# The queries' up product as two row tiles of the array, and the experts' turned rows and sums in one PSUM bank

## The chip, the cores and the metric

The kernel is one program on one core of a Trainium2 chip. Its time is the device time of one execution in microseconds. The engines are PE (TensorE, matmul), ACT (ScalarE), DVE (VectorE), POOL (GpSimd) and SP (SyncE, here the engine that issues most transfers). PSUM, which PE writes and ACT and DVE read, has eight banks of 128 partitions x 512 floats.

## The reference, cut to what matters

Two transformer layers over 4 x 256 tokens of 256 features, in float32. Layer 0 adds an attention and a mixture of experts, both of the same normed input. The parts that the change touches:

```python
xn = _layernorm(x)
# attention of layer 0: 16 heads of 128, through a narrow waist of 64
q = (h @ Wq_c @ Wq_up).reshape(b, t, H, D).transpose(0, 2, 1, 3)   # Wq_c 256x64, Wq_up 64x2048
q = rmsnorm(apply_partial_rope(q, cos, sin), q_norm_w)
... # sliding-window and block attention on q, then two output products
# experts of layer 0: 32 experts, 6 for each token
out += g[:, None] * (jnp.maximum(xf @ w1 + b1, 0.0) @ w2 + b2)      # w1 256x176, w2 176x256
```

Layer 1 has a linear attention and eight experts, two for each token; the change does not alter its work.

## The kernel before

Tokens lie in eight tiles of 128. After a prologue (norms, routing, shared experts, keys) PE, ACT and DVE go through steps g = -1 to 9 in `attention_pe`, `attention_act` and `attention_dve`. In step g the tile g+1 gets its queries, tile g-1 is turned and scored, tile g-2 gets probabilities turned and values, and tile g-3 is projected. A step has eight places: four k places (k = 0 to 3) and four s places (s = 0 to 3, one for each quarter of the tile). Each place also holds one beat of the experts, 79 tiles of 128 gathered rows in a pipeline (`BEATS`, `expert_pe`, `expert_act`). The order is written out by hand and each engine follows its own.

At beat i, PE turns the gathered rows of expert tile i (L865, bank 1), computes the first expert product of tile i-2 (L875, bank 5), and the second, the sums, of tile i-4 (L883 and L884, bank 3, columns 0 to 255). ACT copies the turned rows out (L892), applies the relu (L899, L900), and copies the sums out with the gate as scale (L907). POOL gathers tile i+4 (L837) and adds tile i-4 to the sums in memory (L845); L907 waits for an earlier add to free its buffer.

At place k, in PE's order: the experts' beat, four transposes of tile g-1's queries (`turn_queries`, L499, bank 0), a quarter of the projection (L540, bank 7), one up product of 128 x 512 of tile g+1 (`up_queries`, L486, bank 0), at k=2 the first turned probabilities (L522), and in step 0 a quarter of a fold of two weights (L549). On ACT: the beat, the copy of the turned queries (L592), square and copy of the up product (L586, L587), at k=1 the exponentials of the blocks (L609, L610), at k=2 the copy of turned probabilities (L617). Turned queries and up products share bank 0, so each waits for ACT's copy of the other.

At place s, PE has scores (L511), values (L532), the next turned probabilities (L522), and then the beat; ACT has tanh and exp (L601, L603), the copy of the values (L624), of the turned probabilities (L617), and then the beat. DVE masks and sums there (L698 to L704), and at s=0 sums the squares of all new queries (L665), for which it waits for all four up products' copies.

The up product contracts over 64 features only; the operands `QCT` and `WQ` have 128 partitions, and POOL sets the other 64 to zero in the prologue (L1557, L1558), so that the whole array is used in every matmul. A float32 matmul is two matmul instructions and two weight loads in the trace.

Of the kernel before, what the change touches and what calls it, by code (L numbers as in the profile page):

```python
# [16 lines left out]
P = 128  # L17
B, S, HID = 4, 256, 256
T = B * S
NT = T // P  # L20
# [9 lines left out]
NSUB = 4  # L30
# [94 lines left out]
def build(nc, a, out):  # L125
# [5 lines left out]
    with ctx:  # L131
# [95 lines left out]
        WQC = cut1(KC * QC)  # L227
# [252 lines left out]
        def up_queries(pe, t, k):  # L480

            if t >= 2:
                pe.wait_ge(t_sb, (t - 2) * NG + k + 1)
            else:
                wait(pe, q_ev, t * NG + k)
            nc.tensor.matmul(ps[0][:, :], QCT[:, t * P:(t + 1) * P], wq3[:, k, :], start=True, stop=True).then_inc(q_ps, 1)  # L486

        def turn_queries(pe, t, k):
# [3 lines left out]
            ahead = t + 2 if k else t + 1  # L492
            if ahead < NT:
                pe.wait_ge(q_ev, ahead * NG + (k or NG))
            else:
                wait(pe, t_sb, t * NG + k)
            q3 = v3(QB[t % 2], H)
            for h in range(4):
                ins = nc.tensor.transpose(ps[0][:, h * P:(h + 1) * P], q3[:, 4 * k + h, :], IDN[:, :])  # L499
            ins.then_inc(t_ps, 1)  # L500

        def scores(pe, t, s):
# [5 lines left out]
            for hg in range(NG):  # L508
                if s == 0:
                    pe.wait_ge(t_sb, t * NG + hg + 1)  # L510
# [42 lines left out]
        def attention_pe(pe, g):  # L553
            for k in range(NG):
# [6 lines left out]
                if on(g + 1):  # L561
                    up_queries(pe, g + 1, k)
# [16 lines left out]
        def take_queries(act, t, k):  # L579

            act.wait_ge(q_ps, t * NG + k + 1)
            if k == 0:
                wait(act, qss, t)
                if t == 1:
                    act.wait_ge(x_st, 16)
            nc.scalar.activation(SQ[:, k * 512:(k + 1) * 512], ps[0][:, :], ACT.Square)  # L586
            nc.scalar.activation(QB[t % 2][:, k * 512:(k + 1) * 512], ps[0][:, :], ACT.Copy).then_inc(q_ev, 1)  # L587

        def take_queries_T(act, t, k):

            act.wait_ge(t_ps, t * NG + k + 1)
            nc.scalar.activation(qt4[:, :, 4 * k:4 * k + 4, :].transpose([0, 2, 1, 3]),  # L592
                                 ps[0][:, :].rearrange("p (h s r) -> p h s r", h=4, s=NSUB), ACT.Copy).then_inc(t_sb, 1)
# [36 lines left out]
        def attention_act(act, g):  # L630
            for k in range(NG):
# [4 lines left out]
                if on(g + 1):  # L636
                    take_queries(act, g + 1, k)
# [220 lines left out]
        def expert_pe(pe, i):  # L858

            g = i  # L860
            if g < NT0:
                pe.wait_ge(gathered[g % 4], 16 * (g // 4 + 1))
                wait(pe, xT_sb, g)
                for k in range(KC):
# [14 lines left out]
            if g >= 0:  # L879
                pe.wait_ge(hT_sb, g + 1)  # L880
                wait(pe, y_sb, g)
                w, hT = w2t[g % NW], hT0[g % NHT]
                nc.tensor.matmul(ps[3][:, 0:HID], hT[0:DHB, 0:P], w[0:DHB, 0:HID], start=True, stop=False)  # L883
                nc.tensor.matmul(ps[3][:, 0:HID], hT[0:DHB + 1, P:2 * P], w[0:DHB + 1, HID:2 * HID], start=False, stop=True).then_inc(y_ps, 1)  # L884

        def expert_act(act, i):
# [15 lines left out]
            if g >= 0:  # L902
# [4 lines left out]
                nc.scalar.activation(yt0[g % 2], ps[3][:, 0:HID], ACT.Copy, scale=GY[:, g:g + 1]).then_inc(y_sb, 1)  # L907
# [6 lines left out]
        def turn_tokens(pe, t):  # L914
            pe.wait_ge(xn_ok, NT + t + 1)
            wait(pe, x1t_sb, t - 1)
# [494 lines left out]
        with nc.Block() as block:  # L1411
            @block.sync
            def _(sp):
# [15 lines left out]
                sp.dma_start(WQ[0:QC, :], a["L0_attn_Wq_up"]).then_inc(ld_ct, 16)  # L1429
# [44 lines left out]
                for i in range(NBEAT):  # L1474
# [30 lines left out]
                    if i == NBEAT - 4:  # L1505
                        sp.wait_ge(q_ps, NT * NG)
# [41 lines left out]
            def _(pool):  # L1548
# [8 lines left out]
                ready.link(nc.gpsimd.memset(QCT[QC:, :], 0.0))  # L1557
                ready.link(nc.gpsimd.memset(WQ[QC:, :], 0.0))  # L1558
# [43 lines left out]
            def _(act):  # L1602
# [26 lines left out]
                for n in range(2):  # L1629
                    act.wait_ge(qc_ps, n + 1)  # L1630
                    nc.scalar.activation(QCT[0:QC, n * 512:(n + 1) * 512], ps[4 + n][0:QC, :], ACT.Copy).then_inc(qc_sb, 1)
# [8 lines left out]
                act.wait_ge(const_set, 5 + NHT)  # L1640
# [13 lines left out]
            def _(dve):  # L1654
# [39 lines left out]
                dve.wait_ge(ld_ct, 16 * 4)  # L1694
# [69 lines left out]
            def _(pe):  # L1764
# [160 lines left out]
```

## Time and profile before

| | us |
|---|---|
| median of three runs | 608.5 |
| lowest and highest run | 606.54, 614.78 |
| profiled execution, its time | 607.58 |
| its span | 605.5 |

The profile is of one execution. Busy times are of engines; PE's matmuls overlap at their ends, so that the distance of two starts, not the duration, says what a matmul costs when they follow each other. PEld is the weight load, beside PE. In a timeline row the first number is the start, the second the duration of the group (xN instructions), and the bracket is the idle time of that engine just before and what ended it. The granted clock is TensorE's, as a share of its full speed.

### The profile page before, as it was taken

The numbers are of one execution on the slowest core, as the hardware profiler recorded it, in microseconds if no ns is written. First come the engines' busy times: TensorE is split into PE (matmuls) and PEld (weight loads), VectorE is DVE, ScalarE is ACT, GpSimd is POOL, SyncE is SP. The second block draws the span as 40 slices with busy tenths as digits, with TensorE's granted clock in tenths as the row PEclk, the third lists the DMA queues.
The fourth block names the chain that finished last, engine by engine and source line by source line (L and its number), as shares of the span: only waits on it lengthen the run. The fifth ranks groups of instructions, "written<-read, shape, count | busy, mean of one in ns | idle before, by whom it ended". The sixth has DMA issues, their size and how long they took to land.

```text
span 605.5 us, 9516 instructions
## 1 busy us (share of the span) xinstructions
PE 534.5 (88%) x2887; PEld 403.2 (67%) x2887; DVE 336.9 (56%) x884; ACT 313.0 (52%) x739; POOL 330.7 (55%) x237
## 2 busy tenths in 40 slices
PE   0898999699778999999999999999979998899961
PEld 0654777588566788788787887888757454466641
DVE  3389843324065381743917439151565976998733
ACT  0215226365564766766667666575622228666530
POOL 3100437868667586675866758654311024888770
PEclk9999999899897999999999999999999999999995
DMA  9940628886886986575775757865377012556766
GB/s 286 344 166 6 162 59 208 196 163 174 218 252 164 235 214 141 118 173 120 151 160 118 172 120 156 188 134 112 36 233 236 1 35 62 79 87 94 97 77 216
DMA packets 87200, 90.31 MB, mean 149 GB/s; under 512 B 26672, under 2 KB 75248, under 8 KB 86704
## 3 DMA queue, kind: packets, MB, share of 16 engines
q1 hardware_dynamic: 66528, 61.44, 35.7%
q0 software_dynamic: 19584, 27.24, 26.5%
q10 hardware_dynamic: 1040, 1.05, 0.5%
q8 instruction: 24, 0.39, 0.3%
q14 instruction: 24, 0.20, 0.1%
HBM read 65.25 MB, written 22.60 MB: 145 GB/s over the span
## 4 chain that ended last, share of the span: by engine, by line
PE 56%; DVE 15%; issue 8%; DMA 8%; POOL 7%; ACT 5%; SPq 0%; POOLq 0%; DVEq 0%
PE bank L540 9%; DMA expert_sums<-expert_weights,token_of_slot 6%; PE bank L875 6%; PE bank L1115 4%; PE bank L486 4%; PE bank L883 3%; PE bank L884 3%; POOL expert_sums L845 3%; PE bank L511 3%; POOL expert_weights L837 3%; PE bank L532 3%; PE bank L1785 3%; PE bank L1133 2%; PE bank L499 2%; PE bank L865 1%
## 5 line engine op out<-in xcount | busy, mean ns | idle before, releaser
L845 POOL DMA_INDIRECT expert_sums<-expert_weights,token_of_slot x79 | 129.6, 1641 | 57.9 <-ACT expert_weights L907 35.4
L837 POOL DMA_INDIRECT expert_weights<-normed_x,token_of_slot x79 | 91.8, 1162 | 112.3 <-DVE token_of_slot L366 46.6
L875 PE MATMUL bank<-expert_weights 128*88 128x128 f32 x632 | 83.6, 275 | 0.5 <-issue 0.4
L875 PEld LDWEIGHTS bank<-expert_weights 128*88 128x88 f32 x632 | 74.3, 159 | 0.9 <-issue 0.9
L540 PE MATMUL bank<-out_weights,expert_weights 128*128 128x256 f32 x256 | 60.1, 380 | 1.4 <-ACT expert_weights L624 1.4
L907 ACT ACTIVATE expert_weights<-bank,chosen_bf 128x256 f32<-128x256 f32 x79 | 37.5, 475 | 33.0 <-issue 18.7
L1083 POOL DMA_INDIRECT expert_sums<-expert_weights,token_of_slot x23 | 45.8, 1989 | 14.4 <-DMA expert_sums<-expert_weights,token_of_slot 5.5
L883 PE MATMUL bank<-expert_weights 88*128 88x256 f32 x158 | 48.0, 385 | 6.0 <-ACT expert_weights L907 5.0
L698 DVE SCALAR_TENSOR_TENSOR expert_weights<-bank,blocks_valid 128x64 f32<-128x64 f32 x32 | 7.1, 221 | 81.0 <-ACT expert_weights L601 80.4
L540 PEld LDWEIGHTS bank<-out_weights,expert_weights 128*128 128x128 f32 x256 | 46.5, 190 | 8.2 <-ACT expert_weights L624 3.1
L1076 POOL DMA_INDIRECT tiles<-normed_x,token_of_slot x23 | 25.2, 1097 | 41.6 <-DVE token_of_slot L1070 28.9
L884 PE MATMUL bank<-expert_weights 89*128 89x256 f32 x158 | 47.4, 380 | 0.0
L1115 PE MATMUL bank<-expert_weights,tiles 128*128 x92 | 44.1, 601 | 1.3 <-DVE tiles L1165 0.9
L511 PEld LDWEIGHTS bank<-keys,expert_weights 128*128 128x128 f32 x256 | 33.8, 196 | 14.9 <-issue 13.9
L511 PE MATMUL bank<-keys,expert_weights 128*128 128x112 f32 x256 | 34.7, 280 | 8.4 <-DVE expert_weights L698 8.4
L486 PE MATMUL bank<-q_up_weights,qc_T 128*128 128x512 f32 x64 | 35.4, 635 | 7.3 <-ACT expert_weights L592 5.8
L586 ACT ACTIVATE tiles<-bank 128x512 f32<-128x512 f32 x32 | 19.1, 596 | 42.7 <-PE bank L486 40.3
L853 DVE SCALAR_TENSOR_TENSOR expert_weights<-expert_weights,chosen_before_bf 128x6 f32<-128x6 f32 x79 | 15.9, 222 | 42.9 <-DMA expert_weights<-normed_x,token_of_slot 42.6
L892 ACT ACTIVATE expert_weights<-bank 128x256 f32<-128x256 f32 x79 | 30.3, 384 | 11.9 <-PE bank L865 11.9
L899 ACT ACTIVATE expert_weights<-bank,expert_weights 88x128 f32<-88x128 f32 x79 | 28.8, 364 | 13.2 <-PE bank L875 8.4
L532 PE MATMUL bank<-expert_weights 112*128 112x512 f32 x64 | 33.4, 603 | 2.3 <-ACT expert_weights L617 2.3
L884 PEld LDWEIGHTS bank<-expert_weights 89*128 89x128 f32 x158 | 30.3, 192 | 4.4
(278 smaller groups left out, 1110.3 us busy)
## 6 DMA issues: line engine op xcount, KB each, us to landing
expert_weights<-experts_out SPq DMA_DIRECT2D x79, 192.8 KB
expert_weights<-experts_in SPq DMA_DIRECT2D x79, 176.0 KB
expert_weights<-L_ffn_wi SPq DMA_DIRECT2D x32, 128.0 KB
expert_weights<-w_comp SPq DMA_DIRECT2D x1, 2048.0 KB, 10.9
expert_weights<-fold_g SPq DMA_DIRECT2D x1, 2048.0 KB, 16.2
expert_sums<-zeros SPq DMA_DIRECT2D x2, 1024.0 KB, 13.3
expert_weights<-L_ffn_wo SPq DMA_DIRECT2D x16, 128.0 KB
normed<-expert_sums SPq DMA_DIRECT2D x2, 1024.0 KB, 5.7
```

The costliest lines, as they stand in the source:

```text
L486: nc.tensor.matmul(ps[0][:, :], QCT[:, t * P:(t + 1) * P], wq3[:, k, :], start=True, stop=True).then_inc(q_ps, 1)
L511: ins = nc.tensor.matmul(ps[2][:, hg * NKEY:(hg + 1) * NKEY], QT[:, s * H * NSR + hg * P:s * H * NSR + (hg + 1) * P], kwin[:, b, i, :], st ...
L532: nc.tensor.matmul(ps[6][:, :], VW[b % 2][0:NKEY, i * D:(i + 1) * D], PTB[s % 2][0:NKEY, :], start=True, stop=True).then_inc(pv_ps, 1)
L540: ins = nc.tensor.matmul(ps[7][:, 0:HID], AO[:, h * P:(h + 1) * P], wc3[:, h, :], start=(h == 0), stop=(h == H - 1))
L837: nc.gpsimd.indirect_dma_start(xt0[g % 4], None, xn0, bass.IndirectOffsetOnAxis(ap=MAP[:, g:g + 1], axis=0)).then_inc(gathered[g % 4], 16)
L845: nc.gpsimd.indirect_dma_start(sums0[g % 2], bass.IndirectOffsetOnAxis(ap=MAP[:, g:g + 1], axis=0), yt0[g % 2], None, compute_op=ALU.add). ...
L875: ins = nc.tensor.matmul(ps[5][0:DHB, c * P:(c + 1) * P], w[:, k * DH + c * DHB:k * DH + (c + 1) * DHB], xT0[g % NXT][:, k * P:(k + 1) * P ...
L883: nc.tensor.matmul(ps[3][:, 0:HID], hT[0:DHB, 0:P], w[0:DHB, 0:HID], start=True, stop=False)
L884: nc.tensor.matmul(ps[3][:, 0:HID], hT[0:DHB + 1, P:2 * P], w[0:DHB + 1, HID:2 * HID], start=False, stop=True).then_inc(y_ps, 1)
L907: nc.scalar.activation(yt0[g % 2], ps[3][:, 0:HID], ACT.Copy, scale=GY[:, g:g + 1]).then_inc(y_sb, 1)
L1083: nc.gpsimd.indirect_dma_start(sums1[n % 2], bass.IndirectOffsetOnAxis(ap=MAP[:, g:g + 1], axis=0), yt1[g % 4], None, compute_op=ALU.add). ...
L1115: ins = nc.tensor.matmul(ps[HB[g % 2]][:, :], xT1[g % 3][:, k * P:(k + 1) * P], w[:, 0, k * 2 * MI:(k + 1) * 2 * MI], start=(k == 0), stop ...
```

## The change

- The waist's product is computed twice, side by side: `w_qc` holds `Wq_c` two times, so that `QCT` has the 64 features in partitions 0 to 63 and again in 64 to 127. `WQ` holds the weights of heads 0 to 7 in its first 64 partitions and those of heads 8 to 15 in the other 64, in half the columns. The two memsets are gone.
- `up_queries` runs at k=1 and k=3 only. Each call is four products of 64 rows and 256 columns, in turn from the lower and the upper 64 partitions, into banks 0 and 3. One signal follows the fourth. ACT then takes bank 0 and bank 3, a square and a copy each (`take_queries` with i = 0, 1).
- The queries are turned in the order of head groups 0, 2, 1, 3, with banks 0 and 3 in turn; the scores follow that order.
- To free bank 3, the experts' sums go to columns 256 to 511 of bank 1, whose first half holds the turned rows. PE waits for the previous sum's copy (`y_sb`) ahead of the turned rows, and for this beat's copy of the turned rows (`xT_sb`) ahead of the sums.
- `WQC` lies in the free half of `WQ`; some semaphore counts follow, and PE waits for `slots_ok` ahead of the steps and for the last sum ahead of layer 1's turned tokens.

```diff
-        wq3 = v3(WQ[:, :], NG)
+        QBANK, QORDER = (0, 3), (0, 2, 1, 3)
...
-        def up_queries(pe, t, k):
+        def up_queries(pe, t, j):
 
             if t >= 2:
-                pe.wait_ge(t_sb, (t - 2) * NG + k + 1)
+                pe.wait_ge(t_sb, (t - 2) * NG + 2 * j + 2)
             else:
-                wait(pe, q_ev, t * NG + k)
-            nc.tensor.matmul(ps[0][:, :], QCT[:, t * P:(t + 1) * P], wq3[:, k, :], start=True, stop=True).then_inc(q_ps, 1)
+                wait(pe, q_ev, t * NG + 2 * j)
+            for lo in range(0, 512, HID):
+                for i in range(2):
+                    rows = slice(i * QC, (i + 1) * QC)
+                    ins = nc.tensor.matmul(ps[QBANK[i]][:, lo:lo + HID], QCT[rows, t * P:(t + 1) * P], WQ[rows, j * 512 + lo:j * 512 + lo + HID],
+                                           start=True, stop=True)
+            ins.then_inc(q_ps, 1)
 
         def turn_queries(pe, t, k):
...
-            ahead = t + 2 if k else t + 1
+            ahead, part = (t + 1, 3 + k) if k < 2 else (t + 2, k - 1)
             if ahead < NT:
-                pe.wait_ge(q_ev, ahead * NG + (k or NG))
+                pe.wait_ge(q_ev, ahead * NG + part)
...
-                ins = nc.tensor.transpose(ps[0][:, h * P:(h + 1) * P], q3[:, 4 * k + h, :], IDN[:, :])
+                ins = nc.tensor.transpose(ps[QBANK[k % 2]][:, h * P:(h + 1) * P], q3[:, 4 * QORDER[k] + h, :], IDN[:, :])
...
-                if on(g + 1):
-                    up_queries(pe, g + 1, k)
+                if k % 2 and on(g + 1):
+                    up_queries(pe, g + 1, k // 2)
...
-        def take_queries(act, t, k):
-
-            act.wait_ge(q_ps, t * NG + k + 1)
-            if k == 0:
+        def take_queries(act, t, j, i):
+
+            k = j + 2 * i
+            act.wait_ge(q_ps, t * 2 + j + 1)
+            if i + j == 0:
...
-            nc.scalar.activation(SQ[:, k * 512:(k + 1) * 512], ps[0][:, :], ACT.Square)
-            nc.scalar.activation(QB[t % 2][:, k * 512:(k + 1) * 512], ps[0][:, :], ACT.Copy).then_inc(q_ev, 1)
+            nc.scalar.activation(SQ[:, k * 512:(k + 1) * 512], ps[QBANK[i]][:, :], ACT.Square)
+            nc.scalar.activation(QB[t % 2][:, k * 512:(k + 1) * 512], ps[QBANK[i]][:, :], ACT.Copy).then_inc(q_ev, 1)
...
-                if on(g + 1):
-                    take_queries(act, g + 1, k)
+                if k % 2 and on(g + 1):
+                    for i in range(2):
+                        take_queries(act, g + 1, k // 2, i)
...
@@ expert_pe @@
                 wait(pe, xT_sb, g)
+                wait(pe, y_sb, g - 4)
...
                 wait(pe, y_sb, g)
+                pe.wait_ge(xT_sb, min(i + 1, NT0))
                 w, hT = w2t[g % NW], hT0[g % NHT]
-                nc.tensor.matmul(ps[3][:, 0:HID], hT[0:DHB, 0:P], w[0:DHB, 0:HID], start=True, stop=False)
-                nc.tensor.matmul(ps[3][:, 0:HID], hT[0:DHB + 1, P:2 * P], w[0:DHB + 1, HID:2 * HID], start=False, stop=True).then_inc(y_ps, 1)
+                nc.tensor.matmul(ps[1][:, HID:], hT[0:DHB, 0:P], w[0:DHB, 0:HID], start=True, stop=False)
+                nc.tensor.matmul(ps[1][:, HID:], hT[0:DHB + 1, P:2 * P], w[0:DHB + 1, HID:2 * HID], start=False, stop=True).then_inc(y_ps, 1)
...
@@ turn_tokens, prologue @@
+            pe.wait_ge(y_sb, NT0)
...
-                sp.dma_start(WQ[0:QC, :], a["L0_attn_Wq_up"]).then_inc(ld_ct, 16)
+                for i in range(2):
+                    sp.dma_start(WQ[i * QC:(i + 1) * QC, 0:H * D // 2], a["L0_attn_Wq_up"][:, i * H * D // 2:(i + 1) * H * D // 2]).then_inc(ld_ct, 16)
...
-                ready.link(nc.gpsimd.memset(QCT[QC:, :], 0.0))
-                ready.link(nc.gpsimd.memset(WQ[QC:, :], 0.0))
...
-                        ins = nc.tensor.matmul(ps[4 + n][0:QC, :], wqc3[:, k, :], xnT3[:, k, n * 512:(n + 1) * 512],
+                        ins = nc.tensor.matmul(ps[4 + n][:, :], wqc3[:, k, :], xnT3[:, k, n * 512:(n + 1) * 512],
...
-    c["w_qc"] = rows(g("attn_Wq_c"), KC)
+    c["w_qc"] = rows(np.concatenate([g("attn_Wq_c")] * 2, 1), KC)
```

## Rows read from the trace of the kernel before

**Rows 1.** The page: busy time of each engine, with its share of the span

```profile
PE 534.5 (88%) x2887; PEld 403.2 (67%) x2887; DVE 336.9 (56%) x884; ACT 313.0 (52%) x739; POOL 330.7 (55%) x237
```

**Rows 2.** Windows: start:end, us, busy per engine, granted clock, DMA share, GB/s

```profile
100.00:120.00 20.00, 14.32 (x73) 10.71 (x72) 9.26 (x19) 7.21 (x22) 17.23 (x11) 0.91 0.89 204
...
320.00:360.00 40.00, 39.06 (x242) 32.28 (x241) 21.85 (x60) 27.39 (x68) 26.81 (x18) 1.00 0.61 134
```

**Rows 3.** The chain that ended last, two steps' first projection: start, us, what

```profile
300.82 1.73 PE bank L540 x8
...
338.58 1.73 PE bank L540 x8
```

**Rows 4.** Waits from 85 to 200 us: who for whom, total, times, longest

```profile
DVE expert_weights L853 <- DMA expert_weights<-normed_x,token_of_slot: 40.8, 12, 8.2
```

**Rows 5.** The page's groups: the up product of the queries

```profile
L486 PE MATMUL bank<-q_up_weights,qc_T 128*128 128x512 f32 x64 | 35.4, 635 | 7.3 <-ACT expert_weights L592 5.8
```

**Rows 6.** Timeline, PE across a beat's border: start, us, engine, line

```profile
307.38 1.02 PE L486 MATMUL bank<-q_up_weights,qc_T 128*128 128x512 f32 x2
308.24 0.38 PE L865 MATMUL bank<-ident,expert_weights 128*128 128x128 f32 x2
...
309.34 0.60 PE L883 MATMUL bank<-expert_weights 88*128 88x256 f32 x2
309.77 0.60 PE L884 MATMUL bank<-expert_weights 89*128 89x256 f32 x2
```

**Rows 7.** The same timeline, ACT behind that up product

```profile
308.44 0.60 ACT L586 ACTIVATE tiles<-bank 128x512 f32<-128x512 f32 x1 [1.99 <-PE bank L486]
...
309.41 0.42 ACT L609 ACTIVATE expert_weights<-expert_weights 128x256 f32<-128x256 f32 x1
...
309.82 0.38 ACT L892 ACTIVATE expert_weights<-bank 128x256 f32<-128x256 f32 x1
```

**Rows 8.** Timeline, ACT and PE after the fourth up product of a step

```profile
318.86 0.60 ACT L586 ACTIVATE tiles<-bank 128x512 f32<-128x512 f32 x1 [1.99 <-PE bank L486]
...
319.83 0.50 ACT L601 ACTIVATE expert_weights<-bank 128x384 f32<-128x384 f32 x1
...
321.74 0.39 ACT L892 ACTIVATE expert_weights<-bank 128x256 f32<-128x256 f32 x1
...
321.94 0.60 PE L883 MATMUL bank<-expert_weights 88*128 88x256 f32 x2
```

**Rows 9.** Timeline, last beat of the step and the next beat's first instruction

```profile
332.22 1.12 PE L511 MATMUL bank<-keys,expert_weights 128*128 128x112 f32 x8 [0.94 <-DVE expert_weights L698]
...
334.80 0.38 ACT L892 ACTIVATE expert_weights<-bank 128x256 f32<-128x256 f32 x1
...
335.15 0.60 PE L883 MATMUL bank<-expert_weights 88*128 88x256 f32 x2
...
336.02 0.38 PE L865 MATMUL bank<-ident,expert_weights 128*128 128x128 f32 x2
...
336.22 0.47 ACT L907 ACTIVATE expert_weights<-bank,chosen_bf 128x256 f32<-128x256 f32 x1 [0.25 <-PE bank L884]
```

**Rows 10.** Timeline, PE restarting behind ACT in the stage without project

```profile
159.22 0.60 ACT L592 ACTIVATE expert_weights<-bank 128x512 f32<-128x512 f32 x1
...
159.87 1.13 PE L486 MATMUL bank<-q_up_weights,qc_T 128*128 128x512 f32 x2 [0.69 <-ACT expert_weights L592]
...
161.93 0.60 PE L883 MATMUL bank<-expert_weights 88*128 88x256 f32 x2
...
191.40 1.12 PE L486 MATMUL bank<-q_up_weights,qc_T 128*128 128x512 f32 x2 [0.69 <-issue]
```

**Rows 11.** Timeline, a restart after a longer pause of PE

```profile
154.19 2.08 PE L486 MATMUL bank<-q_up_weights,qc_T 128*128 128x512 f32 x2 [1.81 <-ACT expert_weights L592]
...
157.71 0.60 PE L883 MATMUL bank<-expert_weights 88*128 88x256 f32 x2
```

**Rows 12.** Window of the same stretch

```profile
154.00:157.00 3.00, 2.81 (x7) 1.67 (x8) 0.23 (x2) 0.83 (x3) 2.56 (x2) 0.50 0.81 162
```

More of the change, by code:

```diff
@@ L226, in build @@
         KWR = cut1(D)[0:NB * B]
-        WQC = cut1(KC * QC)
+        WQC = WQ[:, H * D // 2:H * D // 2 + 2 * KC * QC]
         WGS = cut1(H * HID)
@@ L491, in turn_queries @@
                 pe.wait_ge(qn, t + 1)
-            ahead = t + 2 if k else t + 1
+            ahead, part = (t + 1, 3 + k) if k < 2 else (t + 2, k - 1)
             if ahead < NT:
-                pe.wait_ge(q_ev, ahead * NG + (k or NG))
+                pe.wait_ge(q_ev, ahead * NG + part)
             else:
-                wait(pe, t_sb, t * NG + k)
+                wait(pe, t_sb, t * NG + k - 1)
             q3 = v3(QB[t % 2], H)
             for h in range(4):
-                ins = nc.tensor.transpose(ps[0][:, h * P:(h + 1) * P], q3[:, 4 * k + h, :], IDN[:, :])
+                ins = nc.tensor.transpose(ps[QBANK[k % 2]][:, h * P:(h + 1) * P], q3[:, 4 * QORDER[k] + h, :], IDN[:, :])
             ins.then_inc(t_ps, 1)
@@ L507, in scores @@
             b, i = t // TPB, t % TPB * NSUB + s
-            for hg in range(NG):
+            for n, hg in enumerate(QORDER):
                 if s == 0:
-                    pe.wait_ge(t_sb, t * NG + hg + 1)
+                    pe.wait_ge(t_sb, t * NG + n + 1)
                 ins = nc.tensor.matmul(ps[2][:, hg * NKEY:(hg + 1) * NKEY],
@@ L585, in take_queries @@
                     act.wait_ge(x_st, 16)
-            nc.scalar.activation(SQ[:, k * 512:(k + 1) * 512], ps[0][:, :], ACT.Square)
-            nc.scalar.activation(QB[t % 2][:, k * 512:(k + 1) * 512], ps[0][:, :], ACT.Copy).then_inc(q_ev, 1)
+            nc.scalar.activation(SQ[:, k * 512:(k + 1) * 512], ps[QBANK[i]][:, :], ACT.Square)
+            nc.scalar.activation(QB[t % 2][:, k * 512:(k + 1) * 512], ps[QBANK[i]][:, :], ACT.Copy).then_inc(q_ev, 1)
         def take_queries_T(act, t, k):
             act.wait_ge(t_ps, t * NG + k + 1)
-            nc.scalar.activation(qt4[:, :, 4 * k:4 * k + 4, :].transpose([0, 2, 1, 3]),
-                                 ps[0][:, :].rearrange("p (h s r) -> p h s r", h=4, s=NSUB), ACT.Copy).then_inc(t_sb, 1)
+            nc.scalar.activation(qt4[:, :, 4 * QORDER[k]:4 * QORDER[k] + 4, :].transpose([0, 2, 1, 3]),
+                                 ps[QBANK[k % 2]][:, :].rearrange("p (h s r) -> p h s r", h=4, s=NSUB), ACT.Copy).then_inc(t_sb, 1)
         def probs(act, t, s):
@@ L906, in expert_act @@
                 act.wait_ge(gate_ok, g + 1)
-                nc.scalar.activation(yt0[g % 2], ps[3][:, 0:HID], ACT.Copy, scale=GY[:, g:g + 1]).then_inc(y_sb, 1)
+                nc.scalar.activation(yt0[g % 2], ps[1][:, HID:], ACT.Copy, scale=GY[:, g:g + 1]).then_inc(y_sb, 1)
         def in_ring(tiles, length, r):
@@ L1630, in _ @@
                     act.wait_ge(qc_ps, n + 1)
-                    nc.scalar.activation(QCT[0:QC, n * 512:(n + 1) * 512], ps[4 + n][0:QC, :], ACT.Copy).then_inc(qc_sb, 1)
+                    nc.scalar.activation(QCT[:, n * 512:(n + 1) * 512], ps[4 + n][:, :], ACT.Copy).then_inc(qc_sb, 1)
                 shared_relu(4)
@@ L1853, in _ @@
                 expert_pe(pe, 3)
-                pe.wait_ge(ld_ct, 16 * 4)
-                pe.wait_ge(const_set, 5 + NHT)
+                pe.wait_ge(ld_ct, 16 * 5)
+                pe.wait_ge(const_set, 3 + NHT)
                 pe.wait_ge(qc_sb, 2)
@@ L1860, in _ @@
                 pe.wait_ge(ld_wg, 32)
+                pe.wait_ge(slots_ok, 2)
                 for g in range(FIRST_STEP, LAST_STEP):
```

6 lines of the change are left out of this document (3 added, 3 removed).

## The prediction

> **What bounds the kernel now.** I read the page first: PE is busy for 88% of the span, DVE, ACT and POOL for 52 to 56% [rows 1]. Then windows of 20 to 40 us, to see where PE has slack. Between 100 and 120 us it is busy 14.3 of 20 us while POOL is busy 17.2 and the DMA engines 0.89; from 85 to 200 us the gates wait 40.8 us for gathered tiles, so that stretch is paced by gathers and scatter-adds. From about 200 us on PE is full: 39.06 of 40 us, ACT at 27.4 [rows 2, 4]. Last the timeline of one beat there. PE runs without a hole: the up product takes 0.86 (307.38 to 308.24), the next beat's turned rows and first expert product 1.10 (to 309.34), then the expert's output pair starts [rows 6]. So in the attention steps g=2 to 7 (from about 190 us on) a hole in PE is a hole in the total, and a shorter product is a gain. The chain of waits runs through PE's products here, and gives the period of a step of eight beats: the first projection stands at 300.82 and at 338.58, 37.8 us [rows 3].
>
> **The profiled execution** took 607.58 us, its span 605.5; the sum goes against 607.6, 0.9 below the median of 608.5.
>
> **The products.** 32 of them run as 64 instructions of 512 columns [rows 5], 0.43 each, 0.86 a product; a step has four, 3.44 us. Afterwards a step has two groups, each of four products of 64 rows and 256 columns, that is eight instructions. A 256-column instruction occupies 0.43/2 = 0.217 [rows 6]. No row shows two row tiles side by side, so I bound a group. Below: perfect pairing, 4 x 0.217 = 0.87. Above: no overlap, 8 x 0.217 = 1.73, plus a drain of PE at each change of shape; a drain is the tail of a matmul, 0.60 less 0.43 = 0.17 [rows 6], so 2.07. I take 1.2: each product is two instructions on the same rows, which I assume not to run beside each other, so that only the three borders between the tiles can overlap: five slots, 1.08, and about one tail. A step saves 3.44 - 2.4 = 1.04; the bounds are 1.70 saved and 0.70 lost.
>
> The Trainium skill (TensorE: Matmul & The Clock Gate, Part 3) says that matmuls of different row groups start some 4 ns apart; by that a group is the 0.87. The Trainium skill (TensorEngine Tiling (Array Packing), Key Properties) says against the change that a switch of tiling mode drains the engine; by that the tails belong in the sum, twice. No row here shows either.
>
> **ACT's burst, the largest term.** Before, each beat left ACT one bank: L586 and L587, 0.97 together (318.86 to 319.83 [rows 8]). Now k=1 and k=3 leave two banks behind one signal, which comes after the whole group: four evacuations, 1.94. They stand ahead of the next beat's L892 in ACT's queue. That was harmless: nothing in the same beat needed L892. The shared bank changes this, since the expert's output pair now waits for this beat's L892. At k=1: ACT starts 0.20 after the products' end (308.44 against 308.24), needs 1.94, then 0.41 for the blocks' exponentials (309.41 to 309.82 [rows 7]), then L892, 0.39. PE restarts behind ACT 0.15 late: L592 ends at 159.82 and PE starts 0.05 later, and from there to L883 it takes 2.06 where 1.96 is usual [rows 10, 6]. That is 3.09 after the products; PE is there after 1.10. **Hole 1.99.**
>
> At k=3, ACT was without a pause from 318.86 to L892 at 321.74; 0.97 later it ends at 323.10, PE restarts at 323.25 instead of 321.94 [rows 8]. **Hole 1.31.** The following two beats each add 0.18, as below, but the fourth scores waited 0.94 for DVE [rows 9], whose chain moves by 1.31 itself; so 1.31 is what passes. In the last beat L892 ends at 335.18, restart 335.33 against 335.15: **0.18** [rows 9]. The beat after the first turned probabilities, k=2, has the same order, another **0.18**.
>
> **The new wait of the turned rows** for the previous sum: free where attention work lies between two beats. Between the last beat of a step and the first of the next nothing does: L907 starts at 336.22, ends at 336.69, restart 336.84 against 336.02 [rows 9]. **0.82.**
>
> A full step: 1.99 + 1.31 + 0.18 + 0.18 + 0.82 = 4.48 added, 1.04 saved, 3.44 net. There are four (g=3 to 6): **+13.8**.
>
> **g=2** has no projection between turning and up: the four up products wait some 0.7 to 0.8 each for L592 [rows 10], 3.0 in all; two such waits of 0.69 remain. At k=0 the turn covers 0.44 of the wait for L907: 0.20 + 0.47 + 0.15 - 0.44 = 0.38. So 4.48 + 1.38 + 0.38 - 3.0 - 1.04 = **+2.2**. **g=7** has no up products: five beats at 0.18 and 0.82, **+1.7**.
>
> **g=-1 to 1** I take at nothing: gathers and scatter-adds pace them [rows 2, 4], and holes in PE fall into time in which it would wait anyway. In g=0 the fold, eight instructions of 0.216 behind every up group, covers most of the burst. If that cover is thinner, the first step's four full beats cost 0.8 each and g=1 about 2, so +5; if the saved product time shows there, -2.
>
> **At no cost:** the two memsets gone from POOL (it waits for the routing long after), two loads of 64 partitions for one, the doubled weights of the compression (512 columns hide the wider load), the waits for `slots_ok` and, in layer 1, for the last sum: all done long before. Bounds 0.5 either way. The turn order 0, 2, 1, 3 moves nothing: the same copies at the same beats. SP's and POOL's queues issue the same transfers.
>
> **Sum:** 607.6 + 13.8 + 2.2 + 1.7 = 625.3, and 0.9 for the median: **626 us**, 2.9% slower. Two per cent, about what a measurement can tell, ends at 620.7 and 596.3.
>
> **Rivals.**
> *Full pairing, and ACT's second hole absorbed:* groups at 0.87 gain 0.66 a step over my choice, and if PE's hole at k=3 falls into waits for DVE, 1.3 goes too. For it: DVE does hold PE up by 0.94 a step. Against: DVE waits for the same ACT queue. Five steps x 1.96 = 9.8, so 616, within 2%. Its first half is what the Trainium skill's page on the clock gate states, above. Chance 0.24.
>
> *The clock falls at each long hole:* after a pause of 1.81 us the granted clock was 0.50 of full speed, which is the level of 1.2 GHz [rows 11, 12]; from L486 to L883 it took 3.52 instead of 2.06, 1.46 lost. The hole at k=1 is as long. Five of them: +7.3, 633. Against: this is one pause; after those of 0.69 and 0.94 the next products ran at full pace [rows 9, 10], and the hole at k=3 is nearer to these. The Trainium skill (TensorE: Matmul & The Clock Gate, Part 1) has the clock fall after idle time, a rule against the change. Chance 0.14.
>
> *Faster:* the evacuation turns out not to be on PE's path, because PE's work ahead of the output pair outlasts ACT's. It decides where that work exceeds 3.1 us behind a group; it is 1.10 in full steps and 2.8 with a fold. Then all 16 groups show, at 0.87: 16 x 0.85 = 13.6, so 595. Only the order of ACT's queue could be otherwise than I read it. Chance 0.07.
>
> *My forecast*, 618 to 635 by itself: 0.55. Slower 0.55 + 0.14 = 0.69, within 0.24, faster 0.07. The range 611 to 638 leaves out the faster case and the edges of the two outer ones.
>
> **What would show it.** Behind each second group four evacuations of 0.49 run back to back on ACT, and L883 waits for L892 about 2.0 us at k=2 and 1.3 us at the first scores beat; L865 waits 0.8 for L907 once a step; PE's share from 320 to 360 us falls from 0.98 to about 0.88; the period grows from 37.8 to about 41. The start of one group and the next instruction are 1.2 us apart if five slots are right, 0.87 or over 1.7 if not. I am wrong if L883 shows no wait for L892, or if steps g=2 to 7 are no longer while the early stage is.

## The result: 3.5% slower, and the profile after

The median went from 611.42 us (606.54 to 614.78, four runs, taken in the same comparison) to **630.98 us** (628.41 to 631.75, four runs): ratio **1.0354**, 95% interval 1.0317 to 1.0391. The profiled execution took 630.83 us, its span 629.0; before 607.58 and 605.5. So the difference is 19.6 between the medians and 23.5 between the two spans, and the accounts below are of the spans. Ratios leave out the few executions that ran longer at a lower granted clock.

In the kernel after, the up product is L489, turned rows L873, first expert product L883, the sums L892 and L893; on ACT the copy of turned rows is L901, the copy of the sums L916, square and copy of the up product L592 and L593, the copy of the turned queries L598. Experiments have line numbers of their own, a few lines apart.

The page after, busy times as in [rows 1]:

```profile
PE 537.3 (85%) x2951; PEld 404.0 (64%) x2951; DVE 335.1 (53%) x884; ACT 317.7 (51%) x739; POOL 327.2 (52%) x235
```

PE is not busier, only spread over 23.5 us more. The window that answers to the second of [rows 2], and one in step g=2:

```profile
320.00:360.00 40.00, 36.21 (x228) 29.18 (x227) 20.46 (x56) 25.03 (x61) 24.85 (x16) 1.00 0.59 133
204.00:206.00 2.00, 2.00 (x11) 2.00 (x10) 0.00 (x0) 1.45 (x4) 1.41 (x2) 0.50 0.58 174
```

From 320 to 360 us PE's share fell from 39.06 to 36.21 of 40 us at full clock. What it waited for, the whole span (who for whom: total, times, longest):

```profile
PE bank L892 <- ACT expert_weights L901: 19.2, 16, 1.7
...
PE bank L873 <- ACT expert_weights L916: 13.6, 16, 3.7
```

The first line is the new wait: the sums for this beat's copy of the turned rows. The timeline shows how it comes about. First the beat behind the group at k=1 of a full step (start, duration, engine, line; the bracket is the idle time before):

```profile
318.61 1.89 PE L545 MATMUL bank<-out_weights,expert_weights 128*128 128x256 f32 x8
...
320.43 1.13 PE L489 MATMUL bank<-q_up_weights,qc_T 64*128 64x256 f32 x8
321.49 0.44 PE L873 MATMUL bank<-ident,expert_weights 128*128 128x128 f32 x2
321.61 0.60 ACT L592 ACTIVATE tiles<-bank 128x512 f32<-128x512 f32 x1 [2.21 <-PE bank L489]
321.77 1.04 PE L883 MATMUL bank<-expert_weights 128*88 128x128 f32 x8
322.10 0.59 ACT L593 ACTIVATE normed<-bank 128x512 f32<-128x512 f32 x1
322.58 0.60 ACT L592 ACTIVATE tiles<-bank 128x512 f32<-128x512 f32 x1
323.06 0.62 ACT L593 ACTIVATE normed<-bank 128x512 f32<-128x512 f32 x1
323.54 0.44 ACT L615 ACTIVATE expert_weights<-expert_weights 128x256 f32<-128x256 f32 x1
...
323.95 0.40 ACT L901 ACTIVATE expert_weights<-bank 128x256 f32<-128x256 f32 x1
...
324.50 0.67 PE L892 MATMUL bank<-expert_weights 88*128 88x256 f32 x2 [1.69 <-ACT expert_weights L901]
```

From the start of the turned rows behind the group to L892 it takes 321.49 to 324.50, 3.01, where it took 1.10 [rows 6]. Then the group at k=3 and the first scores beat, and the scores and the end of the beat at the last place:

```profile
332.46 1.14 PE L489 MATMUL bank<-q_up_weights,qc_T 64*128 64x256 f32 x8
333.52 1.15 PE L516 MATMUL bank<-keys,expert_weights 128*128 128x112 f32 x8
...
337.51 0.39 ACT L901 ACTIVATE expert_weights<-bank 128x256 f32<-128x256 f32 x1
...
338.04 0.67 PE L892 MATMUL bank<-expert_weights 88*128 88x256 f32 x2 [0.96 <-ACT expert_weights L901]
```

```profile
307.18 1.12 PE L516 MATMUL bank<-keys,expert_weights 128*128 128x112 f32 x8 [0.30 <-DVE expert_weights L705]
...
310.28 0.67 PE L892 MATMUL bank<-expert_weights 88*128 88x256 f32 x2
...
311.42 0.47 ACT L916 ACTIVATE expert_weights<-bank,chosen_bf 128x256 f32<-128x256 f32 x1 [0.50 <-PE bank L893]
312.04 0.41 PE L873 MATMUL bank<-ident,expert_weights 128*128 128x128 f32 x2 [0.66 <-ACT expert_weights L916]
```

Where the time lies, by the starts of the experts' sums on PE (start of tile 8n to start of tile 8(n+1); four full steps together):

| | before | after | difference | forecast |
|---|---|---|---|---|
| up to the first sum | 88.98 | 87.08 | -1.90 | 0 |
| g=-1 | 26.35 | 30.38 | +4.03 | |
| g=0 | 35.51 | 35.03 | -0.48 | |
| g=1 | 38.41 | 39.35 | +0.94 | g=-1 to 1: 0 |
| g=2 | 34.65 | 38.97 | +4.32 | +2.2 |
| g=3 to 6 | 150.95 | 164.76 | +13.81 | +13.8 |
| g=7 | 33.16 | 35.36 | +2.20 | +1.7 |
| behind | | | +0.6 | 0 |

### The profile page after: what moved, and what is told of

Same layout as the page of the kernel before. It is cut to its first block, busy times and chain, and to the rows that moved or that the text cites. A ratio compares the mean times of both kernels' runs of the same rounds, so it can differ in the third digit from the quotient of the medians.

```text
span 629.0 us, 9647 instructions
## 1 busy us (share of the span) xinstructions
PE 537.3 (85%) x2951; PEld 404.0 (64%) x2951; DVE 335.1 (53%) x884; ACT 317.7 (51%) x739; POOL 327.2 (52%) x235
## 3 DMA queue, kind: packets, MB, share of 16 engines
q10 hardware_dynamic: 1040, 1.05, 0.5%
## 4 chain that ended last, share of the span: by engine, by line
PE 63%; DVE 14%; ACT 10%; issue 6%; DMA 5%; POOL 1%; SPq 0%; ACTq 0%; POOLq 0%; DVEq 0%
PE bank L545 9%; PE bank L883 8%; PE bank L892 6%; PE bank L893 5%; PE bank L1125 4%; DMA expert_sums<-expert_weights,token_of_slot 3%; PE bank L516 3%; PE bank L489 3%; PE bank L537 3%; PE bank L873 2%; ACT normed L593 2%; PE bank L554 2%; PE bank L1794 2%; PE bank L1143 2%; PE bank L504 2%
## 5 line engine op out<-in xcount | busy, mean ns | idle before, releaser
L844 POOL DMA_INDIRECT expert_weights<-normed_x,token_of_slot x79 | 89.1, 1128 | 124.7 <-DVE token_of_slot L366 47.6
L883 PE MATMUL bank<-expert_weights 128*88 128x128 f32 x632 | 85.0, 278 | 0.4 <-ACT expert_weights L909 0.4
L883 PEld LDWEIGHTS bank<-expert_weights 128*88 128x88 f32 x632 | 75.6, 161 | 0.7 <-issue 0.7
L892 PE MATMUL bank<-expert_weights 88*128 88x256 f32 x158 | 51.8, 410 | 20.1 <-ACT expert_weights L901 19.2
L916 ACT ACTIVATE expert_weights<-bank,chosen_bf 128x256 f32<-128x256 f32 x79 | 37.6, 475 | 45.6 <-PE bank L893 36.9
L893 PE MATMUL bank<-expert_weights 89*128 89x256 f32 x158 | 47.7, 382 | 0.0
L873 PE MATMUL bank<-ident,expert_weights 128*128 128x128 f32 x158 | 32.0, 285 | 14.3 <-ACT expert_weights L916 13.6
L901 ACT ACTIVATE expert_weights<-bank 128x256 f32<-128x256 f32 x79 | 30.5, 386 | 26.2 <-PE bank L873 26.0
L892 PEld LDWEIGHTS bank<-expert_weights 88*128 88x128 f32 x158 | 24.3, 194 | 28.7 <-issue 28.0
L873 PEld LDWEIGHTS bank<-ident,expert_weights 128*128 128x128 f32 x158 | 19.7, 145 | 28.6 <-issue 26.8
```

Source lines behind the costliest of these rows:

```text
L844: nc.gpsimd.indirect_dma_start(xt0[g % 4], None, xn0, bass.IndirectOffsetOnAxis(ap=MAP[:, g:g + 1], axis=0)).then_inc(gathered[g % 4], 16)
L873: ins = nc.tensor.transpose(ps[1][:, k * P:(k + 1) * P], xt0[g % 4][:, k * P:(k + 1) * P], IDN[:, :])
L883: ins = nc.tensor.matmul(ps[5][0:DHB, c * P:(c + 1) * P], w[:, k * DH + c * DHB:k * DH + (c + 1) * DHB], xT0[g % NXT][:, k * P:(k + 1) * P ...
L892: nc.tensor.matmul(ps[1][:, HID:], hT[0:DHB, 0:P], w[0:DHB, 0:HID], start=True, stop=False)
L893: nc.tensor.matmul(ps[1][:, HID:], hT[0:DHB + 1, P:2 * P], w[0:DHB + 1, HID:2 * HID], start=False, stop=True).then_inc(y_ps, 1)
L916: nc.scalar.activation(yt0[g % 2], ps[1][:, HID:], ACT.Copy, scale=GY[:, g:g + 1]).then_inc(y_sb, 1)
```

## The experiments

Each was timed beside runs of the kernel before on the same chip; a ratio is to these. "Period" is the distance of the sums' starts over a full step (before 37.74, after 41.19; the mean of four steps, in the profiled execution).

### Whole rows instead of row tiles

```diff
-            for lo in range(0, 512, HID):
-                for i in range(2):
-                    rows = slice(i * QC, (i + 1) * QC)
-                    ins = nc.tensor.matmul(ps[QBANK[i]][:, lo:lo + HID], QCT[rows, ...], WQ[rows, ...], ...)
+            for i in range(2):
+                ins = nc.tensor.matmul(ps[QBANK[i]][:, :], QCT[:, t * P:(t + 1) * P], WQ[:, j * 512:j * 512 + 512], ...)
```

> The changed kernel, but each group is two products over all 128 rows and 512 columns into the same two banks, behind the same signal (each query then gets the sum of two head groups' products; this is the part of the computation that is altered). Theory (the loss is ACT's burst and the shared bank, and the row tiles themselves gain): a group costs 1.73 instead of about 1.15 us, some 0.6 in each of 10 to 12 groups on the path, so 631 becomes about 637; the waits of the expert's output pair for the copy of the turned rows stay 2.0 and 1.3 us. Rival (the row tiles cost, by drains at the change of shape): not slower than the changed kernel, 625 to 631.

Measured 644.68 us, ratio 1.054 (1.0495 to 1.0585); the period is 44.15, 2.96 above the kernel after. The row tiles are not what costs. The time is above the 637 that I expected: more went than the products' 1.0, and most of the rest is the clock. PE behind the long hole of this kernel, and a window there:

```profile
335.65 0.67 PE L890 MATMUL bank<-expert_weights 88*128 88x256 f32 x2 [1.82 <-ACT expert_weights L899]
...
336.59 0.95 PE L502 MATMUL bank<-ident,normed 128*128 128x128 f32 x4
337.34 3.26 PE L543 MATMUL bank<-out_weights,expert_weights 128*128 128x256 f32 x8
340.44 0.60 PE L525 MATMUL bank<-ident,expert_weights 128*112 128x128 f32 x4
```

```profile
338.00:340.00 2.00, 2.00 (x6) 1.53 (x6) 0.00 (x0) 0.18 (x1) 1.70 (x2) 0.50 0.71 217
```

Turning and projection take 3.85 (336.59 to 340.44) instead of 2.17 at the same place of the kernel after (325.44 to 327.61). So 1.7 of the 2.96 is the granted clock at 0.50, its lower level of 1.2 GHz; 1.0 is the products, and 0.3 the two long holes, each a little longer (by 0.14 at k=2 and 0.19 at the first scores). The profiled execution was the slowest of five (650.42, mean granted clock 0.962, against 642.28 to 645.91 and 0.972 to 0.978), so the others lost less to the clock than this one.

### The shared bank alone

```diff
 # the kernel before, with nothing changed in the up products
                 wait(pe, xT_sb, g)
+                wait(pe, y_sb, g - 4)
...
+                pe.wait_ge(xT_sb, min(i + 1, NT0))
-                nc.tensor.matmul(ps[3][:, 0:HID], hT[0:DHB, 0:P], ...)
+                nc.tensor.matmul(ps[1][:, HID:], hT[0:DHB, 0:P], ...)
```

> The kernel before with one part of the change, the experts' sums in the second half of bank 1 with both new waits; up products as before. Theory: the expert's output pair waits for this beat's copy of the turned rows even without a burst of four: about 0.6, 1.0, 0.7 and 0.3 us in the four beats behind up products, 0.2 and 0.8 at the end of a step, 3.6 a step, five steps, and 1.7 in the step after: some 20 us, about 629. Rival (the row tiles cost, the bank is free): 606 to 613.

Measured 634.99 us, ratio 1.0392 (1.0351 to 1.0432), period 41.73, +3.99, more than the 3.6 a step and the 629 us that I expected. PE's waits:

```profile
PE bank L885 <- ACT expert_weights L894: 14.2, 30, 0.9
PE bank L866 <- ACT expert_weights L909: 11.4, 12, 2.8
```

This part alone costs as much as the whole change. With one bank of queries left to ACT at each k place the wait comes twice as often (30 times against 16) and is at most 0.9 long: ACT's copy of the turned rows is late in seven of the eight beats of a step, and the pairs gather most of that lateness into two places.

### ACT takes the banks of k=1 behind the copy of the turned rows

```diff
+            def late():
+                for i in range(2):
+                    take_queries(act, g + 1, 0, i)
...
-                    expert_act(act, i)
+                    expert_act(act, i, late if k == 2 and on(g + 1) else None)   # called right behind L901
```

> The changed kernel, but at k=1 ACT takes the two banks behind the next beat's copy of the turned rows instead of ahead of it. Theory: the hole of 2.0 us at k=2 goes, in five steps, and with it the fall of the clock near 205 us: about 619 to 621; the hole of 1.3 at the first scores beat stays. Rival (PE waits for something else there, or another wait takes its place): 628 to 632.

Measured 618.86 us, ratio 1.0128 (1.0088 to 1.0169), period 39.27: 1.92 less. The beat at k=2 in this kernel:

```profile
319.73 1.04 PE L886 MATMUL bank<-expert_weights 128*88 128x128 f32 x8
...
320.73 0.67 PE L895 MATMUL bank<-expert_weights 88*128 88x256 f32 x2
```

Nothing was taken away but the place of four instructions in ACT's queue, and the first of the two holes is gone. That shows it as the cause: same matmuls, same copies, same banks.

### The products not in turn

```diff
-            for lo in range(0, 512, HID):
-                for i in range(2):
+            for i in range(2):
+                for lo in range(0, 512, HID):
```

> The changed kernel, but a group issues both products of the lower rows, then both of the upper rows. Theory of the five slots (instructions of one tile don't overlap, only borders between the tiles do): one border instead of three, seven slots, 1.52 instead of 1.08 us, so a group grows by 0.43 and the total by 4 to 5, about 636. Rival (all overlap, whatever the order; or none does): the same 631.

Measured 628.84 us, ratio 1.0292 (1.025 to 1.0335), not the 636 of the theory of five slots; three full steps take 41.2, and the first takes 42.88. The group takes the same time with both products of the lower rows ahead of both of the upper (318.58 to 319.65):

```profile
318.58 1.14 PE L489 MATMUL bank<-q_up_weights,qc_T 64*128 64x256 f32 x8
319.65 0.44 PE L873 MATMUL bank<-ident,expert_weights 128*128 128x128 f32 x2
```

Cut into its instructions, a group is four pairs in both kernels, and so it is in all 16 groups of each. The two of a pair start 6 to 7 ns apart when issued in turn, and 12 to 14 ns when not. The second pair starts 0.32 behind the first, the next two 0.216 behind each other. In the kernel after, what is left of the group from its third, fifth and seventh instruction on, each row from a narrower window:

```profile
320.75 0.81 PE L489 MATMUL bank<-q_up_weights,qc_T 64*128 64x256 f32 x6
...
320.96 0.60 PE L489 MATMUL bank<-q_up_weights,qc_T 64*128 64x256 f32 x4
...
321.18 0.38 PE L489 MATMUL bank<-q_up_weights,qc_T 64*128 64x256 f32 x2
```

So all eight overlap in twos. "Only the borders between tiles" is wrong, and "in turn" has no part in the gain.

The step of 42.88 is a matter of the clock, behind a hole no longer than those of the other three steps, where the clock stayed at 1.00:

```profile
238.57 0.67 PE L892 MATMUL bank<-expert_weights 88*128 88x256 f32 x2 [1.70 <-ACT expert_weights L901]
...
240.00:242.00 2.00, 2.00 (x7) 1.70 (x6) 0.14 (x2) 0.82 (x2) 1.24 (x2) 0.50 0.42 99
```

### Both pairs moved

The turns go in twos to k=0 and k=2 with the group behind them, and ACT takes each pair of banks one place later, behind the copy of the turned rows:

```diff
+            def turned(k):
+                if k % 2 == 0 and on(g - 1):
+                    turn_queries(pe, g - 1, k)
+                    turn_queries(pe, g - 1, k + 1)
+                if on(g - 3):
+                    project(pe, g - 3, k)
...  # at k=0 turned() stands ahead of the beat, else behind it
-                if k % 2 and on(g + 1):
+                if k % 2 == 0 and on(g + 1):
                     up_queries(pe, g + 1, k // 2)
...  # on ACT
+                    expert_act(act, i, late(k // 2) if k % 2 and on(g + 1) else None)
```

> The changed kernel with its places rearranged: two turns of the queries and the group of products at k=0 and at k=2, ACT takes the two banks at k=1 and k=3 behind the copy of the turned rows, and at k=0 turns and projection stand ahead of the beat. Theory (only ACT's burst ahead of that copy and the uncovered wait for the previous sum cost; the row tiles gain): a full step loses the holes of 2.0, 1.3 and 0.8 us, keeps some 0.2 in the last beat, and gains about 1.2 from the products, so about 1 us a step below the kernel before: 600 to 606. Rival (the shared bank costs wherever it stands): 615 or more.

Measured 607.85 us, ratio 0.9971 (0.994 to 1.0002), period 37.56: the loss is gone, but so is most of the gain, for I had expected 600 to 606 us and a step about 1 us below that of the kernel before. What remains, at each place of scores:

```profile
289.87 1.04 PE L898 MATMUL bank<-expert_weights 128*88 128x128 f32 x8
...
290.97 0.67 PE L907 MATMUL bank<-expert_weights 88*128 88x256 f32 x2
...
292.38 1.12 PE L516 MATMUL bank<-keys,expert_weights 128*128 128x112 f32 x8 [0.30 <-DVE expert_weights L720]
```

L898 to L907 is 1.10 where the work needs 0.88 (321.06 to 321.94 before [rows 8]); ACT's copies of values and probabilities stand ahead of the copy of the turned rows in its queue.

### No squares on ACT

```diff
+            if t == 0:
                 nc.scalar.activation(SQ[:, k * 512:(k + 1) * 512], ps[QBANK[i]][:, :], ACT.Square)
```

> The changed kernel, ACT's squares left out for all tiles but the first (the norms of the queries are then those of the first tile; that is the part left out). Theory: the burst is two copies instead of four operations, 0.97 shorter, so the holes of 2.0 and 1.3 us become 1.0 and 0.3, about 1.9 a step in five steps and no fall of the clock: 619 to 621. Rival (ACT's burst isn't what PE waits for): 630.

Measured 620.54 us, ratio 1.018 (1.0119 to 1.024), period 39.34, 1.85 less. The wait at k=2 fell from 1.69 to 0.71, by the 0.98 of two squares, and the one at the first scores by 0.89:

```profile
315.83 0.67 PE L893 MATMUL bank<-expert_weights 88*128 88x256 f32 x2 [0.71 <-ACT expert_weights L902]
```

Every 0.1 us less on ACT is nearly 0.1 less on PE at these two places, although ACT is busy for only 51% of the span.

### One product on 64 rows, without a partner

```diff
 # the kernel before
-            nc.tensor.matmul(ps[0][:, :], QCT[:, t * P:(t + 1) * P], wq3[:, k, :], ...)
+            nc.tensor.matmul(ps[0][:, :], QCT[0:QC, t * P:(t + 1) * P], wq3[0:QC, k, :], ...)
```

> The kernel before, only with the up product contracting over the 64 partitions that hold data: one row tile, one bank, 512 columns. In the changed kernel the eight instructions of a group start in four pairs some 6 ns apart, whichever way the products are ordered. Theory (a pair is one instruction of each tile): a product on one tile keeps its 0.86 us, perhaps 0.1 to 0.3 for the change of shape, 32 times at most: 608 to 616. Rival (a pair is the two instructions of one 64-row product): a product takes about 0.5 us, 0.35 less in some 24 products on the path: 599 to 603, without any second bank.

Measured 621.12 us, ratio 1.0194 (1.0153 to 1.0235), period 39.18, +1.44, which is 4 x 0.36; 32 x 0.36 is the 11.5 between the medians. That is above both ranges I gave (608 to 616, and 599 to 603 by the rival). Around one such product:

```profile
311.76 1.89 PE L540 MATMUL bank<-out_weights,expert_weights 128*128 128x256 f32 x8
313.59 1.12 PE L486 MATMUL bank<-q_up_weights,qc_T 64*128 64x512 f32 x2
314.64 0.44 PE L865 MATMUL bank<-ident,expert_weights 128*128 128x128 f32 x2
314.91 1.04 PE L875 MATMUL bank<-expert_weights 128*88 128x128 f32 x8
```

Start to start, the projection takes 1.83 instead of 1.73 [rows 3], the product 1.05 instead of 0.86 and L865 0.27 instead of 0.22: 0.34 in all for going to the other shape and back. The two instructions of a lone product don't overlap.

### The copy of the turned rows first in every beat

As with both pairs moved, and at every place L901's counterpart now comes ahead of ACT's copies of the values, at k=3 also ahead of the first turned probabilities':

```diff
                 def run():
+                    if k == 3 and on(g - 2):
+                        probs_T(act, g - 2, 0)
...
+                def take(s=s):
+                    if on(g - 2):
+                        outs(act, g - 2, s)
...
-                    expert_act(act, i)
+                    expert_act(act, i, take)
```

> The rearranged kernel (pairs at k=0 and k=2) with one rule on ACT throughout: the copy of the turned rows goes ahead of whatever else is due in the place (at s places ahead of the copy of the values, at k=3 ahead of the copy of turned probabilities). The rearranged kernel's steps take 37.55 us, with waits of 0.22 us, 0.29 with the restart, left at each s place and 0.1 at k=3. Theory (these waits are on PE's path): a step falls by 0.6 to 0.8 to about 36.9, the step without up products by about 1, in all 4 to 5 us below the rearranged kernel, 602 to 605, ratio to before about 0.99. Rival (DVE's chain through the scores sets the s places, so shorter waits change nothing): steps stay at 37.3 to 37.6 and the total at 607.

Measured **606.27 us**, ratio **0.9935** (0.99 to 0.9971), period 37.01: faster than the kernel before by 0.65%, and the fastest version here. Its window answers to [rows 2]:

```profile
320.00:360.00 40.00, 39.43 (x253) 32.79 (x252) 23.32 (x65) 27.58 (x69) 28.71 (x19) 1.00 0.65 138
```

PE is as full as in the kernel before (39.43 against 39.06), and a step is 0.73 shorter. Not all of the gain comes from there: the first sum starts at 87.26 instead of 88.98, which the missing memsets explain in the main (last experiment).

### The same with whole rows

The edit of the first experiment on the kernel just above.

> The kernel of the run beside it (copy first, pairs at k=0 and k=2), but each group as two products over all 128 rows and 512 columns into the same banks (each query gets the sum of two head groups' products; this is the altered part). What the two row tiles are worth by themselves, with no long hole near them: a group costs 1.71 to 1.73 us instead of 1.20 (four pairs of 0.215 and 0.34 for going to the other shape and back), so a step is 1.0 longer, in five steps and some of the early ones 5 to 6 us. Rival (the 3.0 us a step of the earlier full-row kernel were the row tiles' worth, not the clock's fall): a step 3 longer, 15 in all.

Measured 614.82 us, ratio 1.0058 (1.0023 to 1.0093), period 38.01. The row tiles are worth 38.01 - 37.01 = **1.00 a step**; the clock is at 1.00 here in the window from 320 to 360. The shared bank and the pairs, in this order of ACT's queue, cost 38.01 - 37.74 = 0.27. The medians differ by 8.6, more than the 5 to 6 that the steps give: in the profiled executions 4.1 of the 10.2 between the spans lie behind the last start that the table of steps uses (tile 72), where both kernels issue the same work, at a mean granted clock of 0.93 here and 0.96 there.

### The memsets later

```diff
 # the kernel before
+                pool.wait_ge(xn_ok, NT)      # after all norms
                 ready.link(nc.gpsimd.memset(QCT[QC:, :], 0.0))
```

> The kernel before, with POOL's memsets of QCT and WQ held back until DVE has normed all tokens. In the kernel before, the eight norms of DVE (L398) take 4.86 us beside these memsets, in the changed kernel, without them, 2.67, and the first sum comes 1.9 us earlier. Theory (POOL's memsets slow DVE's norms while both run): the norms take 2.7 us again, the first sum comes 1.5 to 2.2 us earlier than 88.98, and the total falls by 1 to 2, about 608 against 610. Rival (something else in the changed prologue does it, such as the smaller loads): norms at 4.9 us, total as before.

Measured 607.71 us, ratio 0.9958 (0.9923 to 0.9993). The norms beside POOL's memsets, in the kernel before:

```profile
13.25 0.95 POOL L1557 MEMSET qc_T<- 64x1024 f32 x1
13.30 4.86 DVE L398 TENSOR_SCALAR normed<-residual,ln_mean_var,rstd 128x256 f32<-128x256 f32 x8 [2.31 <-POOL rstd L407]
```

and with the memsets held back:

```profile
12.92 2.67 DVE L398 TENSOR_SCALAR normed<-residual,ln_mean_var,rstd 128x256 f32<-128x256 f32 x8 [2.31 <-POOL rstd L407]
...
15.71 0.95 POOL L1558 MEMSET qc_T<- 64x1024 f32 x1 [2.91 <-DVE normed L398]
```

The same eight norms took 2.67 instead of 4.86. The first sum starts at 87.66 (before: 88.98). (The profiled execution took 612.52 in all; its time above the median lies at the end, 200.65 from the sums of tile 72 on, against 197.53 before.) In the three kernels with the memsets where they were it starts at 88.98 to 89.75, in the eight without them at 87.00 to 87.99.

## Why the prediction was right, and by which steps

Forecast 626 us and slower; measured 630.98, inside the range. Against its own profiled execution the sum said +17.7, and the span grew by 23.5. The 5.8 between them are +4.5 in g=-1 to 1, +2.1 in g=2, +0.5 in g=7 and +0.6 behind, less 1.9 in the prologue; that the last of these offsets the others is luck. The full steps, the largest term, were forecast and measured at +13.8.

**What bounds the kernel**: right. From g=2 on every hole of PE came out in the period.

**ACT's burst and the new waits, a full step**: right in place and size. By distances between PE's starts, forecast and measured:

| | forecast | measured |
|---|---|---|
| k=2, sums wait for L901 | 1.99 | 1.90 + 0.07 at the restart |
| first place of scores | 1.31 | 1.23 + 0.07 |
| two middle places of scores, less what the wait for DVE shrank | 0 | 0.61 - 0.61 |
| last beat | 0.18 | 0.18 + 0.07 |
| beat at k=3 | 0.18 | 0.12 + 0.08 |
| L873 waits for L916 | 0.82 | 0.82 |
| beat at k=0 | 0 | 0.03 |
| saved by the products | -1.04 | -1.12 |
| net | 3.44 | 3.45 |

The wait for DVE ahead of the fourth scores went from 0.94 [rows 9] to 0.30 and took up the two middle places, as the forecast had it. Two experiments show the burst as the cause by taking it off: -1.92 by order alone, -1.85 by less work. The shared bank alone brings +3.99. PE's share from 320 to 360 us fell to 0.91, less than to the 0.88 that I named.

**The products**: the size was right by luck, the reason wrong. I had five slots of 0.217 and one tail, 1.2. A group is four full slots, 0.86, and about 0.35 for changing shape and back: 0.09 before it, 0.20 in its own time (0.10 each behind the first and the last pair), 0.06 behind it, or 0.10 where scores follow; 0.34 around the lone product. From the group's start to the next instruction it is 1.06, neither the 1.2 nor the 0.87 that I had named as signs. The Trainium skill (TensorE: Matmul & The Clock Gate, Part 3) has matmuls of different row groups start about 4 ns apart; the trace has 6 to 7 ns in turn and 12 to 14 not in turn, which is next to nothing beside a slot of 216. The Trainium skill (TensorEngine Tiling (Array Packing), Key Properties) has the engine drain when the mode changes; the 0.34 fits that, and is the price that no row of before had. By the first rule alone a group would be the 0.87. The gain, 1.00 a step in the pair of kernels that differ in nothing else, is close to what I took (1.04).

**g=2**: too low, +4.3 for +2.2. Two terms were missing and one was too small. I had the first group wait 0.69 for the turned queries' copy; ACT stood idle for 1.84 ahead of L916, which is ahead of that copy in its queue, and the group waited 2.21. L916 waits for an earlier scatter-add to free its buffer: the one of two tiles before was started by POOL at 190.84 and landed 6.4 later, at 197.2, and L916 starts at 197.31. Then the clock fell. The timeline there:

```profile
197.31 0.47 ACT L916 ACTIVATE expert_weights<-bank,chosen_bf 128x256 f32<-128x256 f32 x1 [1.84 <-issue]
...
198.33 1.13 PE L489 MATMUL bank<-q_up_weights,qc_T 64*128 64x256 f32 x8 [2.21 <-ACT expert_weights L598]
...
202.40 0.67 PE L892 MATMUL bank<-expert_weights 88*128 88x256 f32 x2 [1.69 <-ACT expert_weights L901]
...
203.78 1.02 PE L527 MATMUL bank<-ident,expert_weights 128*112 128x128 f32 x4
...
206.72 0.85 PE L892 MATMUL bank<-expert_weights 88*128 88x256 f32 x2
```

L527 to L892 takes 2.94 where a full step needs 1.65 (327.61 to 329.26), and L892 0.69 instead of 0.51: 1.5 us lost at the lower clock level. The window from 204 to 206 us, above, has it at 0.50. So the rival of the clock came true once of five times. Against these two, the four waits of before were worth 4.0 and not the 3.0 that I took off: in the kernel before the turns of this step take 1.29, 1.39, 1.41 and 1.29 to the next product and each product 0.96, where 0.44 and 0.86 would do. That makes 2.2 + 1.5 + 1.5 - 1.0 = 4.2.

**g=7**: +2.2 for +1.7; five beats at 0.25 instead of 0.18 are 0.35 of the 0.5.

**g=-1 to 1**: +4.5 together, near the upper bound of 5 that I gave, where the sum has nothing. Most is in g=-1, +4.0, and the shared bank alone has +2.4 there (28.75 against 26.35), so the cover by gathers and scatter-adds is thin in that step. The trace shows the main parts. Five times no attention work lies between two beats, and the turned rows wait 0.66 for the previous sum's copy, as in the last beat of a full step: 0.82 each with the restart. Two groups leave a hole of 1.28 for L901, 1.5 each. Some 3.7 of waits that the last beats had before are gone, 1.3 is saved by the products, and 1.1 is the clock at 0.50 in this step's last beat, which in the kernel before comes after the step's end.

**The prologue**: I put the memsets at nothing, for what POOL waits for later. What they cost was not on POOL: they slowed DVE's norms beside them, on the path. -1.9, outside my bound of 0.5; the last experiment shows 1.3 of it.

**The rivals**: full pairing did happen, but its 0.87 was not the price of a group; no hole at k=3 was absorbed, so 616 did not come. The faster case would have needed more than 3 us of PE's work ahead of the sums, and there is 1.1 in the full steps.

## What to carry to other kernels

Where two tenants of one PSUM bank are made to wait for each other's copies, the price of sharing is what stands ahead of these copies in the evacuating engine's queue (3.99 us a step here, and 0.27 with the copy first); put the copy that the matmul engine waits for first, and the rest behind it. An engine at 51% busy can set the time of one at 85%. Two row tiles overlapped in full here, but each visit to the other shape cost 0.35 us, so group the products: a visit of four small products gained 0.5 us, a visit of one lost 0.35.

## What the runs showed of the hardware

- Products of 64 rows on the two halves of the array start 6 to 7 ns apart when issued in turn, and 12 to 14 ns apart when issued one half after the other. Which instruction pairs with which in that order is not settled.
- A lone 64-row product of 512 columns costs 1.20 where the one on 128 rows costs 0.86.
- POOL's two memsets of 64 x 1024 and 64 x 2048 slow DVE's `tensor_scalar` beside them, 4.86 for 2.67 us; three of 32 x 128 beside the same norms, in the kernel after, left them at 2.67. The Trainium skill (GPSIMD Engine Reference, 1. Specifications) says that POOL shares its SBUF interfaces with VectorE and that they contend when VectorE runs in a 2-port perf mode or takes two SBUF inputs; the slowdown fits that, but no run here shows which mode the norms ran in.
- The clock doesn't go by the length of the last hole alone. Holes of 1.69 us in the four full steps of the kernel after left it at 1.00; one of 1.70 in a full step of the kernel not in turn was followed by 0.50, and so was one of 1.69 where a hole of 2.21 had ended 4.1 us earlier. With whole rows the five holes of 1.82 and 1.83 were each followed by a fall in the profiled execution, the slowest of its kernel, and before it was at 0.50 behind 1.81 [rows 11, 12]. Yet longer holes did nothing elsewhere: the one of 2.19 below, in step g=2 of the fastest kernel, has the clock at 1.00 from 198 to 203 us, and one of 2.35 without the squares has it at 1.00 from 185 to 190. What tells these apart was not tried, so each such hole was a risk of some 1.5 us more, not a certainty.

```profile
198.11 1.13 PE L489 MATMUL bank<-q_up_weights,qc_T 64*128 64x256 f32 x8 [2.19 <-ACT expert_weights L604]
```
